# A causal block and six windowed layers on one core: layer changes in small steps, PSUM homes by bank, last residual in the loop

## The reference, cut to what matters

```python
x = L0_attn_x                                   # (8, 512, 128)
mod = (silu(c) @ wmod)                          # sa, ca, ga, sb, cb, gb for each of the 8 batches
h = layernorm(x) * (1 + ca) + sa
x = x + ga * causal_attention(h)                # 16 heads of 64, all 512 positions
h = layernorm(x) * (1 + cb) + sb
y = h
for i in range(6):                              # six layers, each with weights of its own
    q, k, v = shift_tokens(y) @ Wqkv[i]
    q, k = l2norm(q) * q_scale[i], l2norm(k) * k_scale[i]     # then rotary tables on both
    y = windowed_attention(q, k, v) @ Wo[i] + y               # windows of 32, own and previous one
    y = (a * gelu(gate)) @ W2[i] + b2[i] + y                  # a, gate = layernorm(shift(y)) @ W1[i] + b1[i]
return x + gb * y
```

## Time and profile before

| | us |
|---|---|
| median of three runs | 3763.39 (3753.32 to 3766.66) |
| the profiled execution | 3756.22 |
| its span, first to last instruction | 3754.2 |
| TensorE / GpSimd / VectorE / ScalarE busy in the span | 3392.6 / 3107.4 / 2955.4 / 2601.3 |

### The profile page before, as it was taken

One profiled execution on the slowest core, in us unless ns is written; L12 is line 12 of the kernel. 1 busy time (PEld: TensorE's weight loads), 2 busy tenths in 40 slices (PEclk: granted clock), 3 DMA queues, 4 the chain that ended last, 5 costly groups with the idle time before them and its releaser, 6 DMA issues.

```text
span 3754.2 us, 162428 instructions
## 1 busy us (share of the span) xinstructions
PE 3392.6 (90%) x72292; PEld 2052.2 (55%) x72292; DVE 2955.4 (79%) x3116; ACT 2601.3 (69%) x3315; POOL 3107.4 (83%) x2468
## 2 busy tenths in 40 slices
PE   7999999589998999989999889999899998989995
PEld 4666666355554555555555555555455555555553
DVE  7888887677887887878777778777788787887774
ACT  6777776467776666776677766776766777767773
POOL 3555556589998999989899988999899998989992
PEclk9999999799999999999999999999999999999997
DMA  1000000244545454545454544454444454545442
GB/s 62 5 5 8 5 5 24 75 112 114 122 107 118 95 117 108 117 109 116 93 127 108 117 100 106 114 122 105 113 102 110 116 116 106 119 95 116 104 108 80
DMA packets 162053, 347.53 MB, mean 93 GB/s; under 512 B 32588, under 2 KB 42064, under 8 KB 155088
## 3 DMA queue, kind: packets, MB, share of 16 engines
q1 hardware_dynamic: 161360, 337.15, 38.4%
HBM read 24.54 MB, written 4.19 MB: 8 GB/s over the span
## 4 chain that ended last, share of the span: by engine, by line
PE 50%; POOL 12%; DVE 7%; issue 6%; ACT 5%; SPq 1%; DMA 0%; DVEq 0%; POOLq 0%; ACTq 0%
PE psB L673 26%; PE psA L673 21%; POOL sq L1387 3%; PE psB L730 2%; DVE h L1289 2%; PE psA L730 1%; ACT sq L980 1%; POOL pb L1407 1%; POOL h L1382 1%; POOL h L1383 1%; POOL f_c L1412 1%; DVE ts L1281 1%; POOL n_a L1397 1%; POOL n_a L1394 1%; POOL n_b L1402 1%
## 5 line engine op out<-in xcount | busy, mean ns | idle before, releaser
L1362 POOL TENSOR_TENSOR pt<-wk,pt 128x256 f16<-128x256 f32 (+3 forms) x256 | 368.2, 1455 | 284.1 <-ACT pt L903 194.5
L1387 POOL TENSOR_TENSOR sq<-sq 128x512 f32<-128x512 f32 x384 | 487.3, 1281 | 82.7 <-ACT sq L980 82.4
L1382 POOL TENSOR_TENSOR h<-h,ts 128x512 f32<-128x512 f32 x384 | 503.1, 1310 | 35.3 <-DVE ts L1281 35.3
L1383 POOL TENSOR_TENSOR h<-h,ts 128x512 f32<-128x512 f32 x384 | 496.9, 1294 | 0.0
L1407 POOL TENSOR_TENSOR pb<-pb,rc 128x1024 f32<-128x1024 f32 x192 | 365.5, 1904 | 63.2 <-DVE rc L1302 60.5
L1300 DVE TENSOR_REDUCE sum<-pb 128x16 f32<-128x1024 f32 x192 | 232.9, 1213 | 108.5 <-ACT pb L1013 108.5
L1273 DVE TENSOR_TENSOR h<-psB,t_rot 128x1024 f32<-128x1024 f32 x192 | 233.6, 1217 | 77.1 <-ACT sq L980 72.6
L673 PE MATMUL psA<-kf,qf 64*32 64x64 f32 x18432 | 250.7, 227 | 29.3 <-issue 28.0
L980 ACT ACTIVATE sq<-psA 128x1024 f32<-128x1024 f32 x192 | 196.1, 1022 | 109.3 <-PE psA L673 109.2
L1273 DVE TENSOR_TENSOR h<-psA,t_rot 128x1024 f32<-128x1024 f32 x192 | 233.5, 1216 | 35.4 <-DMA kf<-h 13.9
L980 ACT ACTIVATE sq<-psB 128x1024 f32<-128x1024 f32 x192 | 196.2, 1022 | 88.2 <-PE psB L673 87.7
(11 more groups left out here) (364 smaller groups left out, 11040.7 us busy)
## 6 DMA issues: line engine op xcount, KB each, us to landing
qf<-h SPq DMA_DIRECT2D x768, 136.0 KB
kf<-h SPq DMA_DIRECT2D x768, 136.0 KB, 2.8
vev<-vo SPq DMA_DIRECT2D x192, 256.0 KB
vev<-vo SPq DMA_DIRECT2D x192, 224.0 KB
stage<-wqk SPq DMA_DIRECT2D x12, 512.0 KB, 5.3
stage<-wvl SPq DMA_DIRECT2D x12, 256.0 KB, 5.5
stage<-wof SPq DMA_DIRECT2D x6, 512.0 KB, 4.7
xb<-xt SPq DMA_DIRECT2D x8, 256.0 KB, 7.9
```

What stands on the lines that cost most here:

```text
L1362: e.tensor_tensor(pt[g][pr][:, :, 1, o:o + w], wk[(slot_of(s)[0] - 1) % SLOTS][:, :, 0:w], pt[g][pr][:, :, 0, o:o + w], ALU.subtract).then ...
L1382: e.tensor_tensor(halves_of(h, 0), halves_of(h, 0), t[1], ALU.subtract)
L1383: e.tensor_tensor(halves_of(h, 1), halves_of(h, 1), t[0], ALU.add).then_inc(ended["ad"])
L1387: e.tensor_tensor(sqb[c][:, 0, :], sqb[c][:, 0, :], sqb[c][:, 1, :], ALU.add).then_inc(ended["qa"])
```

## The change

- The order tables of all five engines are new.
- **Tables by four.** `tb` is four steps, one for each of q or k and cosine or sine, two activations each; a step waits for the last `tc` (cosine) or `ts` (sine) of the old layer on that table alone, and only the first new `tc` or `ts` that reads it waits for it.
- **Weights by pieces.** `stage` is four buffers of 512 columns. A layer's weights are eight pieces (0 to 2 the first half of the heads, 3 to 5 the second, 6 and 7 the output weights), each with its own `wh`/`wl` or `oh`/`ow`; piece p lies in buffer p % 4 and SP refills it by an `st` step.
- `wf` 0 and 1 (`w1h`, `w1l`) and `ws` 0 and 1 (`w2h`, `w2l`) are steps of the `VECTOR` table instead of calls behind `fm` and `fr`. The first layer's too.
- **PSUM homes.** `plan_banks`: a step has a fixed home pair, A to D, and a one-bank step takes one half of it (`l` or `r`).
- Ahead of the first layer the clearing memsets are on POOL, and the second half's first weights (`wl -1 1 1`) stand ahead of the first `tc` on DVE.
- **Last residual in the loop.** In the last layer `kept` (the `t_tab` quarters and the four `stage` buffers) receives x from HBM one batch at a time during the first four batches; `fr` becomes four instructions, two before the wait for `fo` (gb times the residual plus x) and two after it from PSUM. The 16 instructions at the end are gone.

```diff
-    "fm0 bm12 bm13 tc01+1 ts01+1 fm2 tc03+1 ol10 ts03+1 tc02+1 wl1 ts02+1 ol11 fm1 mx00+1 tc10+1 ts10+1 sm00+1 mx01+1 "
+    "ws1 ol00+3 tc13+3 ts13+3 wl01+4 wl00+4 wf0+1 wl10+3 mx10+3 wl02+3 wf1+1 mx11+3 sm10+3 tc00+4 sm11+3 ts00+4 "
...
+ONE_BANK = ("ss", "op", "la", "fo")
+def plan_banks(steps, homes):
+    user, place = [None] * 8, {}
+    for s in steps:
+        if s in homes:
+            at = 2 * "ABCD".index(homes[s][0]) + (homes[s][1:] == "r")
+            own = range(at, at + (1 if s[0] in ONE_BANK else 2))
+            place[s] = (at, sorted({user[i] for i in own if user[i]}))
+            for i in own:
+                user[i] = s
     return place
...
-        stage = sb("stage", [128, 1536])
+        stage = [sb(f"stage{i}", [128, 512]) for i in range(4)]
...
                 if kind == "st":
-                    li = v // (2 * NB) + 1
-                    e.wait_ge(*done("wl", v))
-                    if v % 2 == 0:
-                        heads_of(e, li, 1)
+                    p = s[2]
+                    e.wait_ge(*done("wl", v, (p - 4) // 3, (p - 4) % 3))
+                    piece_of(e, (v + 1) // NB, p)
...
+                if li == L - 1 and u < NB:
...
+                    e.wait_ge(s_x1d[u], 16)
+                    e.dma_start(kept[u], x1d[u]).then_inc(s_x1d[u], 16)
...
                 elif kind == "tb":
-                    li = v // (2 * NB)
+                    k, h = divmod(s[2], 2)
+                    li = v // NB
                     e.wait_ge(s_tab, 32)
                     if li:
-                        e.wait_ge(*all_done("ts", *((v - 1, x) for x in range(4))))
-                    for k in range(2):
-                        for h in range(2):
-                            for y in range(2):
-                                p = e.activation(t_rot[:, k, h, y, :], t_tab[:, 2 * k + h, :], ACT.Copy,
-                                                 scale=t_scl[:, li, 2 * k + y:2 * k + y + 1])
-                    p.then_inc(ended["tb"])
+                        e.wait_ge(*all_done("ts" if h else "tc", *((2 * v - 1 - x, k + 2 * i) for x in range(2) for i in range(2))))
+                    e.activation(t_rot[:, k, h, 0, :], t_tab[:, 2 * k + h, :], ACT.Copy, scale=t_scl[:, li, 2 * k:2 * k + 1])
+                    e.activation(t_rot[:, k, h, 1, :], t_tab[:, 2 * k + h, :], ACT.Copy, scale=t_scl[:, li, 2 * k + 1:2 * k + 2]
+                                 ).then_inc(ended["tb"])
...
+        def weights_low(e, v, x, j):
+
+            e.wait_ge(*done("wh", v, x, j))
+            e.scalar_tensor_tensor(out=head_weights(1, x, j), in0=stage[(3 * x + j) % 4][:, :], scalar=WS,
+                                   in1=head_weights(0, x, j), op0=ALU.mult, op1=ALU.subtract).then_inc(ended["wl"])
...
                 elif kind == "fr":
                     b, li = v % NB, v // NB
                     o = psum(("fo", v))
+                    if li == L - 1:
+                        y = kept[b]
+                        e.wait_ge(s_x1d[b], 32)
+                        e.scalar_tensor_tensor(out=y[0:64, :], in0=xb[0:64, b, 0:S], scalar=t_mod[0:64, 5, b:b + 1],
+                                               in1=y[0:64, :], op0=ALU.mult, op1=ALU.add).then_inc(s_y)
...
+                        e.wait_ge(*done("fo", v))
+                        e.scalar_tensor_tensor(out=y[0:64, :], in0=o[0:64, 0:512], scalar=t_gz[0:64, b:b + 1], in1=y[0:64, :],
+                                               op0=ALU.mult, op1=ALU.add).then_inc(s_z)
...
-            for b in range(NB):
-                y = sqb[b // 2][:, b % 2, :]
-                e.scalar_tensor_tensor(out=y[0:64, :], in0=xb[0:64, b, 0:S], scalar=t_mod[0:64, 5, b:b + 1], in1=y[0:64, :],
-                                       op0=ALU.mult, op1=ALU.add)
```

More of the change, by code:

```diff
@@ L318, in program @@
         t_gs = sb("t_gs", [128, L])
+        t_gz = sb("t_gz", [128, NB])
+        kept = [t_tab[:, b, :] for b in range(4)] + [t[:, :] for t in stage]
         x1d = nc.dram_tensor("x1_keep", [NB, 128, S], F32).ap()
@@ L415, in psum @@
         def psum(s):
-            return pair[place[s][0]]
+            at = place[s][0]
+            return pair[at // 2][:, 512 * (at % 2):512 * (at % 2) + 512] if s[0] in ONE_BANK else pair[at // 2]
         def made(v, c):
@@ L462, in sync @@
                         e.wait_ge(*full(("c_op", b)))
[L463 removed]
+                        for p in range(4):
+                            piece_of(e, 0, p)
                         e.dma_start(flat(t_tab), tab).then_inc(s_tab, 16)
@@ L675, in take @@
             def take(s):
-                slot, before = place[s]
-                if before:
+                for before in place[s][1]:
                     k, at = before[0], before[1:]
@@ L762, in local_tensor @@
                     e.wait_ge(*done("xl", v // 2))
-                    e.wait_ge(ended["wl"], 2 * li + half + 1)
+                    if b == 0:
+                        e.wait_ge(*done("wl", v // 2 - 1, half, c // 2))
                     x = [xs[b % 2][z][:, :] for z in range(2)]
@@ L794, in local_tensor @@
                     e.wait_ge(*done("xl", v // 2))
-                    e.wait_ge(ended["wl"], 2 * li + half + 1)
+                    if b == 0:
+                        e.wait_ge(*done("wl", v // 2 - 1, half, 2))
                     for c in range(4):
@@ L1267, in local_vector @@
                     c = s[2]
-                    e.wait_ge(ended["tb"], v // (2 * NB) + 1)
+                    if v // 2 % NB == 0:
+                        e.wait_ge(*done("tb", v // 2, c % 2 * 2))
                     e.wait_ge(*done("sq", v, c))
```

249 lines of the change are left out of this document (130 added, 119 removed), and 21 rows, old and new, of tables (SCALAR, TENSOR, VECTOR).

## The result

The changed kernel takes 3651.27 us (median of four, 3642.16 to 3660.93) against 3764.34 in the same runs: a ratio of 0.9706, 95% interval 0.9671 to 0.9740, 113 us less. The forecast was 3637, 126 less, in a range of 3575 to 3705. Its profiled execution took 3642.16, the shortest of the four, so its windows are some 9 us in all shorter than the median's.

A forecast was written before the change was run, and what follows sets the result against it. GpSimd and TensorE were taken to bound quiet iterations, with layer changes adding 160 us. Terms -120 (changes), 0 (loop), +6 (start), -12 (end) sum to -126, giving 3637 us from the median; range 3575 to 3705.

The forecast's parts named there:

- Layer changes, -120: Five layer changes: put at 160 us in all, 32 each; 8 of each stays, so 120 us gained, bounds 60 to 160.
- The new loop, 0: Every iteration, new order and fixed PSUM homes: bounds -1.5 to +1.5 us each, -72 to +72 in all, taken as 0.
- a shorter loop: Rival: one-bank homes remove TensorE's waits in every iteration, -1.5 us by 48, total 3565 us; chance 0.14.
- Tables: ScalarE's table activations at a layer change: four portions of 1.4 us; 3 of the first window's 14.8 extra us stay.
- Weights by pieces: Attention weight splits at a layer change: eight pieces fit VectorE's spare time; 1 to 2 us of a change stay.
- the rival: Pieces meet GpSimd: each of eight takes 1.70 us, 20 of 32 us stay per change, total 3697; chance 0.18.
- w1 and w2: Feed-forward weight splits on VectorE: worst instructions stay, one `w1h` 3.14, three `w2h` 1.31; 3 of 10 us stay per change.
- the 60 to 63 given as a sign: Sign of being right: iterations at a layer change take 60 to 63 us, with the clock near 1.00 throughout.
- Start, +6: Start of the layer stage: first `tc` at 687.5 behind a DMA-fed piece, plus GpSimd clearing; +6 us, bounds 0 to +10.
- End, -12: Kernel end: output leaves right after the last PSUM instructions, -12 us; two extra 0.75 us instructions per iteration in VectorE's spare time.
- slower: Rival: tight homes bind in every iteration and late scores hold back GpSimd; iterations of 62 us, total 3786; chance 0.08.
- no effect: Rival: a change's cost is refilling behind any wait at the lower clock; only the end's 12 less 6 remain, 3757; chance 0.07.

## Why the prediction held, point by point

- **What bounds the loop**: right in that GpSimd and TensorE share the chain, and the quiet iteration of 58.4 us is as before. But the best iteration stood for all of them, and so the room in the others was not seen (next points).
- **Layer changes, -120**: the number was right (-121), by two errors that cancelled. The five changes did not cost 160 but 126 to 136: the step that failed is the base of 58.9 us taken from fourteen chosen iterations, where the loop without any layer work needs 59.4, and the 160 was set above the 149 that even this base gives. What stays was right, 8 a change forecast, 8 to 9 measured. By themselves the changes gained 86 to 90, not 120; the 35 of the next point made up the rest, so the near hit of the total is in part luck.
- **The new loop, 0**: mis-sized. It is 35 us shorter, within the bounds of -72 and +72 but not at 0. I had weighed the homes by their tight places alone and did not find the gain; the weight of 0.14 on a shorter loop was low. It gained though GpSimd was at 97% in the best iteration, which had been the argument against it.
- **Tables**: the mechanism was right, the rank wrong. Left out of the kernel before they are worth 22 us, the attention weights 59; in the new order their cutting is worth 41. A chain shows what stood there, not what takes its place once it is gone.
- **Weights by pieces**: the rival priced each at 1.70 us. They took 0.68 to 1.86, with medians of 1.04 (`wql`) and 0.68 (`wvtl`).
- **w1 and w2**: the last iteration of a change, which holds the w2 splits, is the longest left, 63.9 us in the mean against 58.5 without layer work; three of the five are above the 60 to 63 given as a sign, and the clock is 0.95 in one. Mis-sized: `w1h` was put at 3.14 and took 1.25, and the iteration that holds it is an ordinary one. Not foreseen: the low halves of w2, cheap behind the high ones while GpSimd was idle, wait for GpSimd each on their own in their new place.
- **The rule of the port pair**: the Trainium skill, SBUF — State Buffer, section "Who interferes with whom", has the pair taken for a whole instruction by whichever of VectorE and GpSimd starts first, and ScalarE outside of it. The traces agree: a `w2h` of 0.22 us takes 1.30 beside GpSimd and 0.30 every time on ScalarE, and where VectorE's `wql` starts first, GpSimd's `f_gl` takes 2.14 instead of 1.16. The rival that it stood beside was priced too high: 8 to 9 us of a change stayed, not 20.
- **Start, +6**: +9 in the profiled pair, 7 between the two means of 895 and 888. The first `tc`, forecast at 687.5, was at 686.68. One detail was wrong: it is the third and fourth projection, not the second, that wait for a `ts`. The largest clearing on GpSimd takes 1.80, at the low end of the 1.8 to 5.1:

```profile
679.64 1.80 POOL L1403 MEMSET vev<- 128x2048 f32 x1
```

- **End, -12**: right at its place (3.3 us instead of 15.6), and wrong as a term, since "in VectorE's spare time" did not hold: the last layer paid 11.5 back.
- The rivals "slower" (it wanted longer quiet iterations; the four ahead of each change are 57.8 to 59.9) and "no effect" did not happen. The five stretches of eight iterations are 474 to 478 us, as the sign for "right" wanted (475 to 480).

## What to carry to other kernels

Work that comes once per layer costs by the place and length of its blocks, even where the engine has spare time for all of it: cut it so that it can stand between the other steps, and spread it over iterations. To price it, leave it out and time the kernel; quiet iterations picked from a trace make the price too high. On VectorE put the fewest possible instructions that read two SBUF tensors or run as copies beside a busy GpSimd, and move them to ScalarE where it has room: there each one's wait counts more than its columns. Look for the price on GpSimd too: an instruction of VectorE that gets in first makes GpSimd's longer, and here GpSimd is one of the two engines that set the loop.
